# Batch-norm and layer-norm sweep over the nodes: the additions move from VectorE and GpSimd into matrix products that accumulate in PSUM

## What is computed

```
x = _layernorm(x + _L0_gnn_ref(x, ...))     # three GCN convolutions, each with + x0 and a batch norm
x = _layernorm(x + _L1_gnn_ref(x, ...))     # EVE
x = _layernorm(x + _L2_gnn_ref(x, ...))     # SAGE
x = _layernorm(x + _L3_gnn_ref(x, ...))     # GAT

def _batchnorm(x, gamma, beta):
    mean = jnp.mean(x, axis=0)
    var = jnp.mean(jnp.square(x - mean), axis=0)
    return (x - mean) * jax.lax.rsqrt(var + BN_EPS) * gamma + beta
def _layernorm(x, axis=-1, eps=1e-05):
    return (x - mean(x)) / jnp.sqrt(var(x) + eps)
```

## Times and profile before

| | us |
|---|---|
| median of 3 runs | 11874.25 |
| lowest and highest run | 11871.91, 11890.56 |
| profiled execution, its own time | 11859.96 |
| its span | 11858.0 |
| TensorE busy | 5876.6 (50%) |
| VectorE busy | 7105.0 (60%) |
| ScalarE busy | 4602.1 (39%) |
| GpSimd busy | 7955.8 (67%) |
| TensorE's mean granted clock (1 is full speed) | 0.761 |

### The profile page before, as it was taken

The page is one execution under the profiler, slowest core; times in us unless marked ns, Lnnn a source line. Parts: engine busy times, 40 slices in busy tenths (PEclk is TensorE's granted clock), DMA queues, the critical chain, the costliest instruction groups (busy, mean ns, idle before and its releaser), DMA issues. The chain is left out here.

```text
span 11858.0 us, 164901 instructions
## 1 busy us (share of the span) xinstructions
PE 5876.6 (50%) x34202; PEld 4924.9 (42%) x34203; DVE 7105.0 (60%) x16762; ACT 4602.1 (39%) x8555; POOL 7955.8 (67%) x7679
## 2 busy tenths in 40 slices
PE   1005666666577640166656664655455543334442
PEld 1005665666566630055544443555455422222221
DVE  3335555555455569855547775444466657777776
ACT  1111221222232235444335554333355535555555
POOL 4657776777677754477777775777677665655562
PEclk9998887888788765587777777777787766666665
DMA  5997776888698877577657775766688723333232
GB/s 140 224 188 228 258 264 205 294 298 294 226 310 307 290 253 245 196 241 240 224 192 268 260 260 174 268 242 240 225 308 287 261 81 105 108 103 105 94 94 77
DMA packets 1864914, 2570.40 MB, mean 217 GB/s; under 512 B 255774, under 2 KB 1369142, under 8 KB 1864663
## 3 DMA queue, kind: packets, MB, share of 16 engines
q1 hardware_dynamic: 1134168, 1627.27, 41.8%
q10 hardware_dynamic: 504726, 564.87, 14.5%
q0 software_dynamic: 225792, 375.94, 10.0%
HBM read 1499.62 MB, written 1129.98 MB: 222 GB/s over the span
## 5 line engine op out<-in xcount | busy, mean ns | idle before, releaser
L990 POOL DMA_INDIRECT sums_gcn<-m_result,m_idx x1176 | 1274.9, 1084 | 434.5 <-issue 353.7
L982 POOL DMA_INDIRECT m_rows<-node_rows_a,m_idx x1176 | 1218.2, 1036 | 339.6 <-issue 336.8
L1124 ACT ACTIVATE m_nodeT<-m_n_turn 128x512 f32<-128x512 f32 x980 | 568.6, 595 | 1756.4 <-PE m_n_turn L1097 1752.5
L1029 PE MATMUL m_e_turn<-k_ident,m_rows 128*128 128x128 f32 x2744 | 560.9, 343 | 1380.1 <-DMA m_rows<-node_rows_b,m_idx 874.4
L1097 PE MATMUL m_n_turn<-k_ident,m_in_y 128*128 128x128 f32 x5488 | 984.9, 336 | 517.1 <-DMA m_in_y<-node_rows_b 135.9
L990 POOL DMA_INDIRECT sums_eve<-m_result,m_idx x784 | 845.1, 1078 | 360.5 <-issue 233.0
L1029 PEld LDWEIGHTS m_e_turn<-k_ident,m_rows 128*128 128x128 f32 x2744 | 431.4, 180 | 1527.5 <-DMA m_rows<-node_rows_b,m_idx 858.6
L1097 PEld LDWEIGHTS m_n_turn<-k_ident,m_in_y 128*128 128x128 f32 x5488 | 767.4, 172 | 704.7 <-issue 441.5
L982 POOL DMA_INDIRECT m_rows<-node_rows_b,m_idx x784 | 833.4, 1063 | 226.5 <-issue 223.7
L990 POOL DMA_INDIRECT sums_sage<-m_result,m_idx x784 | 787.0, 1004 | 275.7 <-issue 235.0
L2151 POOL DMA_INDIRECT sums_gat<-g_result,g_idx x392 | 416.7, 1063 | 782.3 <-DVE g_result L2411 668.7
(11 more groups left out here) (290 smaller groups left out, 16884.6 us busy)
## 6 DMA issues: line engine op xcount, KB each, us to landing
m_in_sums<-sums_gcn SPq DMA_DIRECT2D x291, 512.0 KB
m_in_y<-node_rows_a SPq DMA_DIRECT2D x291, 512.0 KB
sums_gcn<-k_gcn_b SPq DMA_DIRECT2D x194, 512.0 KB
node_rows_a<-m_y ACTq DMA_DIRECT2D x194, 512.0 KB
m_in_x<-in_x_dram SPq DMA_DIRECT2D x194, 512.0 KB
m_in_y<-node_rows_b SPq DMA_DIRECT2D x194, 512.0 KB
sums_eve<-k_eve_b SPq DMA_DIRECT2D x194, 512.0 KB
m_in_sums<-sums_eve SPq DMA_DIRECT2D x194, 512.0 KB
```

Source lines behind the costliest of these rows:

```text
L982: pool.indirect_dma_start(self.rows[b][:, t, :], None, self.table[:, :], bass.IndirectOffsetOnAxis(self.idx[s][:, t:t + 1], 0)).then_inc(s ...
L990: pool.indirect_dma_start(self.node_sums[:, :], bass.IndirectOffsetOnAxis(self.idx[s][:, T + t:T + t + 1], 0), self.result[b][:, t, :], No ...
L1029: mm = pe.transpose(bank[:, n * P:(n + 1) * P], self.rows[b][:, H * (i % 2) + n, 0:D], self.k["ident"][:, :])
L1124: act.activation(out, src, ACT.Copy).then_inc(self.n_turn_read, 1)
```

## The change

GpSimd has no work in n3 any more. TensorE sums each chunk in two PSUM banks of 512 columns (four slots each), with six products of 512 columns: two multiply a row of ones by the shift row (this opens the sum), two multiply the identity by x0, and two multiply the identity by the scaled y. There are four such pairs of banks, so all eight banks are in use; chunk c uses number c mod 4. VectorE still scales y into z, but no longer adds. Its statistics read the banks, and they are one pair behind: it scales the chunks of pair m and then takes the statistics of pair m-1. ScalarE reads the banks too. Before TensorE opens the sum of chunk c, ScalarE must have read chunk c-4 (`out_ready`). The load program is the same; `z_done` is now given by TensorE's last product of a chunk, which frees the buffer of x0 as well as the z buffer.

```diff
-        shifted, scaled, z_done = ph.sem("shifted"), ph.sem("scaled"), ph.sem("z_done")
+        banks = [[ph.ps(f"sum{i}{h}", [P, HALF]) for h in range(2)] for i in range(4)]
+        scaled, z_done = ph.sem("scaled"), ph.sem("z_done")
...
-                    pool.tensor_tensor(x, x, spread_slots(shift_row[0:n, :], [n, T, D]), ALU.add).then_inc(shifted, 1)
...
+                def unit(m, par):
+                    for c, b, i, n in chunks(m, par):
+                        if not isinstance(m, int) or m >= 2:
+                            pe.wait_ge(ph.out_ready, c - 3)
+                        for h in range(2):
+                            pe.matmul(banks[i][h][0:n, :].rearrange("p (t f) -> p t f", f=D), k["ones"][0:1, 0:n],
+                                      spread_slots(shift_row[0:1, :], [1, H, D]), start=True, stop=False)
+                        ph.have(pe, "x0", b, m)
+                        for h in range(2):
+                            pe.matmul(banks[i][h][0:n, :], k["ident"][0:n, 0:n], ph.buf["x0"][b][0:n, h * H:(h + 1) * H, :].rearrange("p t f -> p (t f)"),
+                                      start=False, stop=False)
+                        pe.wait_ge(scaled, c + 1)
+                        for h in range(2):
+                            mm = pe.matmul(banks[i][h][0:n, :], k["ident"][0:n, 0:n],
+                                           z[i][0:n, h * H:(h + 1) * H, :].rearrange("p t f -> p (t f)"), start=False, stop=True)
+                        mm.then_inc(z_done, 1)
...
+                def statistics(m, par):
+                    for c, b, i, n in chunks(m, par):
+                        dve.wait_ge(z_done, c + 1)
+                        for j in range(T):
+                            ins = dve.bn_stats(ln.stats[0:n, b * T + j, :], tile_of(i, j, n))
+                    ins.then_inc(ln.step, 1)
+                    ln.solve(dve, m, copy=par)
...
                         if not isinstance(m, int) or m >= 2:
-                            dve.wait_ge(ph.out_ready, c - 3)
+                            dve.wait_ge(z_done, c - 3)
                         dve.tensor_tensor(z[i][0:n, :, :], ph.buf["y"][b][0:n, :, :], spread_slots(scale_row[0:n, :], [n, T, D]),
                                           ALU.mult).then_inc(scaled, 1)
-                        dve.wait_ge(scaled, c + 1)
-                        dve.wait_ge(shifted, c + 1)
-                        dve.tensor_tensor(z[i][0:n, :, :], z[i][0:n, :, :], ph.buf["x0"][b][0:n, :, :], ALU.add).then_inc(z_done, 1)
-                    for c, b, i, n in chunks(m, par):
-                        dve.wait_ge(z_done, c + 1)
-                        ins = ln.take(dve, z[i], n, b * T)
-                    ins.then_inc(ln.step, 1)
-                    ln.solve(dve, m, copy=par)
+                    if not isinstance(m, int) or m >= 1:
+                        statistics(m - 1, 1 - par)
...
-                        ln.apply(act, o[i], z[i], n, b * T, copy=par).then_inc(ph.out_ready, 1)
+                        for j in range(T):
+                            at = b * T + j
+                            ins = act.activation(o[i][0:n, j, :], tile_of(i, j, n), ACT.Identity, bias=ln.shift[par][0:n, at:at + 1],
+                                                 scale=ln.scale[par][0:n, at:at + 1])
+                        ins.then_inc(ph.out_ready, 1)
```

More of the change, by code:

```diff
@@ L801, in chunks, with tile_of @@
                 yield 2 * m + b, b, 2 * par + b, sh.rows(2 * m + b)
+        def tile_of(i, j, n):
+            return banks[i][j // H][0:n, (j % H) * D:(j % H + 1) * D]
         with nc.Block() as block:
@@ L806, in _ @@
                 ph.load_program(sp, {"y": [(scaled, 1)], "x0": [(z_done, 1)]})
[L808 to L813, removed]
-                    pool.tensor_tensor(x, x, spread_slots(shift_row[0:n, :], [n, T, D]), ALU.add).then_inc(shifted, 1)
-                ph.node_sweep(pool, step)
+            @block.tensor
+            def _(pe):
+                def unit(m, par):
[14 more added lines that the diff above has]
+                        mm.then_inc(z_done, 1)
+                pair_units(pe, unit)
             @block.vector
             def _(dve):
+                def statistics(m, par):
[5 more added lines that the diff above has]
+                    ln.solve(dve, m, copy=par)
                 def unit(m, par):
@@ L823, in unit @@
                         if not isinstance(m, int) or m >= 2:
-                            dve.wait_ge(ph.out_ready, c - 3)
+                            dve.wait_ge(z_done, c - 3)
                         dve.tensor_tensor(z[i][0:n, :, :], ph.buf["y"][b][0:n, :, :], spread_slots(scale_row[0:n, :], [n, T, D]),
                                           ALU.mult).then_inc(scaled, 1)
-                        dve.wait_ge(scaled, c + 1)
-                        dve.wait_ge(shifted, c + 1)
-                        dve.tensor_tensor(z[i][0:n, :, :], z[i][0:n, :, :], ph.buf["x0"][b][0:n, :, :], ALU.add).then_inc(z_done, 1)
-                    for c, b, i, n in chunks(m, par):
-                        dve.wait_ge(z_done, c + 1)
-                        ins = ln.take(dve, z[i], n, b * T)
-                    ins.then_inc(ln.step, 1)
-                    ln.solve(dve, m, copy=par)
+                    if not isinstance(m, int) or m >= 1:
+                        statistics(m - 1, 1 - par)
                 pair_units(dve, unit)
+                statistics(pairs - 1, (pairs - 1) % 2)
             @block.scalar
```

## The result

| | us |
|---|---|
| before, median of 4 runs | 11879.58 (11871.91 to 11890.56) |
| after, median of 4 runs | 11729.98 (11715.5 to 11748.84) |
| ratio after / before, 95% interval | 0.9874 [0.9856, 0.9893] |
| profiled execution of after: its own time, span | 11720.86, 11717.5 |

The change makes the kernel 150 us faster. The forecast was 11732, so the total came out within 2 us of it. The first thing to do with such a number is to ask whether the gain lies where it was put. I cut both profiled executions at the same events: the first load of n3, the first instruction of the phase behind it, and the first one of the GAT phase.

A forecast was written before the change was run, and what follows sets the result against it. VectorE was taken to bound n3 at 12.76 us a pair; afterwards a ring of waits, with DMA close, would give 9.8. Gain 142 us: 11860 - 142 = 11718, median 14 above, so 11732 us; range 11685 to 11812.

The forecast's parts named there:

- VectorE loses 2.4 us of additions and 3.0 us of standing still: VectorE in n3: additions go and waiting beside GpSimd ends; it then needs 8.2 us a pair.
- A statistics instruction costs 0.26 us from PSUM: VectorE's 16 statistics in n3: 4.2 us a pair reading PSUM, 1.0 more than before.
- ScalarE stays at 7.8 us a pair: ScalarE in n3: unchanged at 7.8 us a pair from PSUM, a bound only if all else falls below.
- Twelve products take 5.2 us at 2.4 GHz and 11.0 at 1.2: TensorE in n3: 0.43 or 0.92 us a product by clock; 3.5 us taken for a chunk's six.
- The clock: TensorE's granted clock in n3: taken as 0.75 on average, up from 0.50.
- Rival (b): TensorE in n3 stays at its low clock: 11.3 us a pair, gain 71 us, 11803 us; chance 0.19.
- The ring: Longest chain of waits in n3, through two pairs, ScalarE, TensorE, loads and VectorE: 19.25 us, 9.6 a pair.
- The first root comes 2.4 us later: Start of n3: the second pair is scaled before the first statistics, one more landing of y, 2.4 us net.
- What would show it: Signs in n3's profile: roots 9.8 us apart, VectorE idle 1.5 us a pair, clock near 0.75, DMA share near 0.9.
- The other phases keep their code: Phases outside n3: nothing changes there, so the whole gain of 142 us comes from n3.
- (c): TensorE's weight loads in n3 no longer hidden: 15.0 us a pair, 102 us slower, 11976 us; chance 0.03.
- (d): n3 unchanged: low clock, 6.8 us landing and 2 us of late landings, 12.5 to 13.1 us a pair; chance 0.03.

The follow-up runs named there:

- before_no_gpsimd: Kernel before without GpSimd's addition of the shift, which is not added at all; ratio 0.9862, n3 499.8 us, 9.91 us a pair.
- no_shift: Kernel after without the two shift-row products of each chunk, 8 products a pair instead of 12; ratio 0.9993, n3 507.6 us.
- shift_twice: Kernel after with each chunk's two shift-row products done twice, 16 products a pair instead of 12; ratio 1.0277, n3 940.0 us.
- x0_twice: Kernel after with each chunk's two x0 products (128 rows) done twice, 16 products a pair; ratio 1.0018, n3 733.9 us.
- dve_adds_even: Kernel after with VectorE adding x0 to the even chunk of each pair, 10 products a pair; ratio 0.9900, n3 553.1 us.
- dve_adds_x0: Kernel after with VectorE adding x0 to both chunks of each pair, 8 products a pair; ratio 0.9862, n3 522.6 us.

## Why the prediction came out right, point by point

- *VectorE loses 2.4 us of additions and 3.0 us of standing still.* Right: L851 at 1225 ns, L703 at 187 ns, and before_no_gpsimd alone gave 2.9 us a pair. GpSimd has no instruction in n3.
- *A statistics instruction costs 0.26 us from PSUM.* Wrong, though harmless: 16 take 3.26 us, 0.20 each, against 3.18 from SBUF. The upper end came from an instruction with other operands. The Trainium skill's 58 against 120 cycles (page "VectorE: DVE Perf Modes", TRN2 errata) doesn't show in the distance between two of them; their mean durations, 283 and 276 ns, differ by 7 ns.
- *ScalarE stays at 7.8 us a pair.* It is a little faster from PSUM, 3.60 us for 10 slots instead of 3.95. It never bound.
- *Twelve products take 5.2 us at 2.4 GHz and 11.0 at 1.2.* This is the step that failed. The terms were read from rows marked x2 as two products, and each row is one product in two records. Read so, the rows give 12 x 0.86 = 10.3 us at the full clock and 12 x 1.83 = 22.0 at the low one. In n3 a product took 0.92 us at the full clock; why not 0.86, no run shows. With its 11.08 a pair TensorE binds: the gain is 612.7 - 10.2 - 47 x 11.08 = 82 us, which is n3's measured 80, and the total would have been forecast as 11792. The clock was missed as well, taken as 0.75 and granted at 0.99; the two errors work against each other, and still the six products of a chunk took 5.54 us and not 3.5. Rival (b)'s pace (11.3) nearly came true by a cause that it did not name.
- *The ring gives 9.6, the pace is 9.8.* Not what bound here, but about right when TensorE was relieved: no_shift ran at 9.91. y landed 5.9 us after its issue, inside the assumed 3.5 to 6.8.
- *The first root comes 2.4 us later.* It came 3.8 later (20.9 us after the first load instead of 17.1), 1.4 us more. Six products of 5.54 us instead of 3.5 stand in its way, which is likely the cause.
- *What would show it.* Two signs spoke for the forecast and were no proof: VectorE idle for y ahead of L851 (184.7 us, 3.8 a pair and not 1.5) and y landing within 6.8 us. The first comes from TensorE's pace, handed on by the queue. The roots (11.03 and not 9.8), the clock (0.99 and not 0.75) and the DMA share (0.81 and not 0.9) spoke against it.
- *The other phases keep their code, so nothing changes there.* The code is the same and the time is not. GAT gave 64 us, and by luck this is what made the total right: 80 + 64 + 21 - 25 = 140 us between the two profiled executions, against 142 forecast from n3 alone. That 12 instructions in VectorE's list turn that phase from 2302.5 to 2369.5 us is shown on one chip, and agrees with the table, which comes from others. On chip B the phase went the other way, and nothing was left of the total gain.
- *Weight loads out of cover (c), no change (d).* Neither. The loads lie beside the products (166 us of PEld beside 439 of PE).

What stays open: why the list's length matters, and why the GAT phase goes the other way on chip B (2650.6 to 2775.9 us), where g_pre's stop shrinks just the same (27.8 to 4.8 us). VectorE's list does not settle the phase's time there: shift_twice has that of after and took 2749.5 us, no_shift has it too and took 2776.0.

For the clock, the share of the products that have one row of weights puts the kernels with a busy TensorE in one order: 4 of 16 (x0_twice) 0.99, 4 of 12 (after) 0.99, 4 of 10 (dve_adds_even) 0.91, 4 of 8 (dve_adds_x0) 0.80, 8 of 16 (shift_twice) 0.77. The claim rests on the two pairs with equal numbers of products, 16 and 8. In dve_adds_even and dve_adds_x0 TensorE also has some idle time (16 and 26 of 440 us), and how much of their fall is due to it is not separated. Nor is the share of such products separated from their standing in a row: eight records in shift_twice, four in the others.

Of the versions that ran, dve_adds_x0 has the shortest n3 with the whole computation in TensorE's banks, 522.6 us against 561.0. The ratio, 0.9862 against 0.9874, doesn't separate it from after. before_no_gpsimd, which leaves out the shift, reaches 499.8 without TensorE and without GpSimd. A version that found a place for the shift beside VectorE's 9.9 us a pair might come near that n3; none ran.

## What to carry to other kernels

Before pricing an operation, find a row for a single one whose count is known from the code, and see how many records it leaves; a price per record is off by that factor. When work moves to an idle engine, its time at the full clock must be under that of the engine it relieves: here 11.1 us a pair against the 9.9 that VectorE took once GpSimd was out of its way. And cut the span into phases before believing a total: an edit can move a phase that it doesn't touch by as much as the one that it does, and repeating both kernels on another chip shows it.

## What the runs showed of the hardware

- A float32 product of 512 columns left two records and took 0.92 us in all in n3, at a granted clock of 0.99 (twelve in a pace of 11.03 us).
- TensorE without idle time had a granted clock of 0.77 in shift_twice, with half its products of one row of weights, and 0.99 in x0_twice, with a quarter; the same number of products. With 8 a pair it was 0.80 with half of them one-row and 0.94 with none.
- VectorE's instruction with two SBUF inputs stands still beside GpSimd's: 1983 ns with it, 1225 ns without.
- With 12 more instructions in VectorE's list its stops at the end of a node part were 3.02 us instead of 0.52, and the GAT phase was 67 us longer (2369.5 and 2302.5).
- Two of the chips ran the convolutions m4 to m7 some 45% slower (6625 and 6520 us against 4513), and one of them this streaming stage as fast as the first (645.0 and 560.9 us against 641.1 and 561.0).
